# Graph attention on one core: the first batch's value blocks in bank pairs of their own, and the weights of layers two and three folded in later slots

## The reference, cut to what matters

```
xl   = x @ W1                                   # 4 heads of 128
e    = leaky_relu(asrc[:, None] + adst[None])   # asrc, adst: xl times two vectors per head
attn = softmax(where(adj > 0 or diagonal, e, -1e9), over sources)
h    = elu(attn^T @ xl + b1)                    # layer one, 4 heads
h    = attention of the same form with W2, one head of 256, + b2      # layer two
x    = layernorm(x + h)
x    = layernorm(x + leaky(softmax(masked leaky(s_i + s_j)) @ (x @ W3)))   # layer three
```

## Time and profile before

| | us |
|---|---|
| median of 3 runs | 977.99 |
| lowest, highest | 976.63, 978.44 |
| the profiled execution's own time | 977.93 |
| its span | 976.1 |

### The profile page before, as it was taken

One profiled execution on the slowest core, in us unless ns is written; L12 is line 12 of the kernel. 1 busy time (PEld: TensorE's weight loads), 2 busy tenths in 40 slices (PEclk: granted clock), 3 DMA queues, 4 the chain that ended last, 5 costly groups with the idle time before them and its releaser, 6 DMA issues.

```text
span 976.1 us, 17256 instructions
## 1 busy us (share of the span) xinstructions
PE 882.8 (90%) x6220; PEld 820.9 (84%) x6220; DVE 740.5 (76%) x1876; ACT 684.9 (70%) x1269; POOL 276.1 (28%) x255
## 2 busy tenths in 40 slices
PE   5687889999999999999999999999999999998653
PEld 4676879998999989898999989898999989897542
DVE  5657697888888887888888888888888888974430
ACT  2466858787786868787786868777786868775530
POOL 1001001124242314224242314224242314224353
PEclk9997999999999999999999999999999999999787
DMA  6303030202102030302102030302102010000000
GB/s 205 111 3 87 1 87 2 87 1 63 48 28 82 22 87 1 109 1 64 46 28 82 22 88 1 108 2 65 45 29 80 23 23 1 23 1 23 22 22 22
DMA packets 62716, 45.04 MB, mean 46 GB/s; under 512 B 35748, under 2 KB 54308, under 8 KB 62632
## 3 DMA queue, kind: packets, MB, share of 16 engines
q1 hardware_dynamic: 62632, 43.93, 15.3%
HBM read 27.14 MB, written 8.39 MB: 36 GB/s over the span
## 4 chain that ended last, share of the span: by engine, by line
PE 36%; DVE 29%; ACT 24%; issue 9%; POOL 2%; POOLq 0%; DMA 0%; SPq 0%; DVEq 0%; ACTq 0%
DVE junk L749 9%; PE bU L478 7%; PE bU L457 7%; PE bG L540 6%; PE bG L526 6%; ACT att L620 6%; ACT att L609 6%; ACT x L632 5%; DVE att L793 3%; PE bB L417 3%; DVE y_lo L786 3%; DVE low L762 3%; DVE y L774 3%; ACT att L624 2%; PE bU L468 2%
## 5 line engine op out<-in xcount | busy, mean ns | idle before, releaser
L749 DVE CUSTOM_DVE_ANT_0 junk<-mask_t,bA,val 128x512 bf16<-128x512 bf16 x320 | 219.8, 743 | 44.7 <-PE bA L417 38.2
L457 PE MATMUL bU<-val,att 128*128 128x129 f32 x2048 | 249.7, 275 | 3.3 <-DVE att L793 3.3
L457 PEld LDWEIGHTS bU<-val,att 128*128 128x128 f32 x2048 | 241.5, 192 | 5.7 <-issue 3.4
L793 DVE SCALAR_TENSOR_TENSOR att<-mask_n,att 128x2048 f32<-128x2048 bf16 x80 | 183.4, 2292 | 81.3 <-ACT att L620 81.3
L609 ACT ACTIVATE att<-bB,val 128x512 f32<-128x512 f32 x320 | 202.4, 707 | 1.3 <-PE bB L417 1.3
L620 ACT ACTIVATE att<-att 128x2048 f32<-128x2048 f32 x80 | 155.2, 1940 | 0.7
L478 PE MATMUL bU<-val3s,att 128*128 128x256 f32 x512 | 118.0, 385 | 11.8 <-POOL val3s L372 11.3
L468 PE MATMUL bU<-val,att 128*128 128x257 f32 x512 | 119.9, 388 | 9.4 <-DVE att L793 9.4
L478 PEld LDWEIGHTS bU<-val3s,att 128*128 128x128 f32 x512 | 96.2, 192 | 27.0 <-issue 13.4
L468 PEld LDWEIGHTS bU<-val,att 128*128 128x128 f32 x512 | 96.6, 194 | 23.7 <-DVE att L793 9.9
L672 ACT COPY val<-bG 128x524 f32<-128x524 f32 x64 | 38.7, 604 | 108.6 <-PE bG L540 108.6
(11 more groups left out here) (87 smaller groups left out, 1585.4 us busy)
## 6 DMA issues: line engine op xcount, KB each, us to landing
adj_in<-in_adj_dram SPq DMA_DIRECT2D x16, 1024.0 KB, 5.8
x_in<-in_x_dram SPq DMA_DIRECT2D x16, 512.0 KB, 6.7
out_dram<-act SPq DMA_DIRECT2D x16, 512.0 KB, 2.9
mask_t<-mask_n SPq DMA_TRANSPOSE x64, 2.5
att<-in_L_gnn_W_dram SPq DMA_DIRECT2D x4, 128.0 KB, 3.1
att<-in_L_gnn_W_dram SPq DMA_DIRECT2D x1, 512.0 KB, 7.4
w<-in_L_gnn_W_dram SPq DMA_DIRECT2D x1, 256.0 KB, 7.6
att<-in_L_gnn_a_dram SPq DMA_DIRECT2D x1, 256.0 KB, 7.3
```

The source lines that it names most:

```text
L457: ins = nc.tensor.matmul(to[:, (d % 2) * FX:(d % 2 + 1) * FX], p[:, s, d * P:(d + 1) * P], val1[u.batch % 2][:, s, u.index // 2, values], ...
L749: nc.vector.tensor_tensor_reduce(junk[:, b] if u.row else att[u.slot % 3][:, b], mask_t[u.batch % 4][:, b], bA[:], 1.0, a_col(u, b) if u.r ...
L793: nc.vector.scalar_tensor_tensor(flat(p), mask_n[u.batch % 3][:, 0:NB * N], BIG, flat(p), ALU.add, ALU.min)\
```

## The change

1. `fold_1` waits for each of the two spread vectors separately, and within each half of W1 it takes the four folds of the first vector before the four of the second.
2. For batch 0, blocks 1 and 2 of the values go to two pairs of banks made of bU0 to bU3, and wait for no copy. Blocks 0 and 3 stay in bG.
3. W2 is loaded into the buffer val3 and the vectors of layers two and three into val3s, instead of att1 and att2.
4. `fold_23` is cut in two. `fold_2` (eight folds) stands in slot 0 at the end of DVE's list, behind `x_low` of batch 1. `fold_3` (the low part of W2 and four folds) stands in slot 2 behind `keep_edges`.
5. ACT's copy `w2_hi` moves from slot -1 to the end of slot 1.
6. `weight_sums` moves from slot 0 to slot 3 on PE and into a bank of bG; `shift_bias_2` moves from slot 0 to slot 4 on DVE.

```
-        bU = [psum(f"bU{i}") for i in range(4)]
+        bUU = [psum(f"bUU{i}", 1024) for i in range(2)]
+        bU = [bUU[i // 2][:, (i % 2) * 512:(i % 2 + 1) * 512] for i in range(4)]
...
+        w2 = val3[:]
+        rows = val3s[:].rearrange("p k n -> p (k n)")
...
-        u_uses = [(colsum_out, 2)]
+        u_uses = []
...
             def values_1(n, b):
                 pe.wait_ge(x_lo_ready, n + 1)
+                apart = n == 0 and b in (1, 2)
                 for g in range(G):
-                    g_wait(g)
-                    to = g_bank(g)[:, 0:HX]
+                    if not apart:
+                        g_wait(g)
+                        g_free[g] = ((val1_ready, n * NB + b + 1),)
+                    to = (bU[2 * b - 2 + g] if apart else g_bank(g))[:, 0:HX]
...
             def weight_sums():
+                g_wait(0)
...
+                g_free[0] = ((colsum_out, 2),)
...
-                if g == 0:
+                if g == 3:
                     weight_sums()
...  (ACT)
-                if g == -1:
-                    act.wait_ge(folded, 2 * KD * H + G + 2 * KH)
-                    nc.scalar.copy(w2_hi[:], w2).then_inc(w2_hi_ready, 1)
...  (ACT, end of the slot, behind elu_exp)
+                if g == 1:
+                    act.wait_ge(folded, 2 * KD * H + G + 2 * KH)
+                    nc.scalar.copy(w2_hi[:], w2).then_inc(w2_hi_ready, 1)
...  (DVE, fold_1)
-                dve.wait_ge(rows_spread, 2)
+                    for i, vectors in enumerate((att1s, att1d)):
+                        dve.wait_ge(rows_spread, i + 1)
...  (DVE, the slots)
-                if g == -3:
-                    fold_23()
...
-                if g == 0:
+                if g == 4:
                     shift_bias_2()
...
                 if this and this.row:
                     keep_edges(this)
+                if g == 0:
+                    fold_2()
+                if g == 2:
+                    fold_3()
```

More of the change, by code:

```diff
@@ L143, in gat_kernel @@
         w1 = att[0][:].rearrange("p b n -> p (b n)")[:, 0:KD * G * HX].rearrange("p (k g n) -> p k g n", k=KD, g=G)
-        w2 = att[1][:].rearrange("p b n -> p (b n)")[:, 0:KH * DX].rearrange("p (k n) -> p k n", k=KH)
-        rows = att[2][:].rearrange("p b n -> p (b n)")
-        row1s, row1d = rows[0:1, 0:HF], rows[0:1, HF:2 * HF]
+        row1s, row1d = (att[2][0:1, i, :] for i in range(2))
         att1s, att1d = bU[0], bU[1]
-        att2s, att2d = rows[:, 2 * HF:2 * HF + DO], rows[:, 2 * HF + DO:2 * HF + 2 * DO]
-        att3 = rows[:, 3 * HF:3 * HF + 2 * DO]
+        w2 = val3[:]
+        rows = val3s[:].rearrange("p k n -> p (k n)")
+        att2s, att2d, att3 = rows[:, 0:DO], rows[:, DO:2 * DO], rows[:, 2 * DO:4 * DO]
         b1_in = x1[0]
@@ L541, in values_1 @@
                                                    stop=(k == KD - 1 and i == 2))
-                    g_free[g] = ((val1_ready, n * NB + b + 1),)
                 ins.then_inc(val1_done, 1)
@@ L546, in weight_sums @@
                 pe.wait_ge(folded, 2 * KD * H + G + 2 * KH)
+                g_wait(0)
                 for k in range(KH):
-                    ins = nc.tensor.matmul(bU[0][:, 0:DX], ones[:], w2[:, k], start=(k == 0), stop=(k == KH - 1))
+                    ins = nc.tensor.matmul(g_bank(0)[:, 0:DX], ones[:], w2[:, k], start=(k == 0), stop=(k == KH - 1))
                 ins.then_inc(colsum_done, 1)
+                g_free[0] = ((colsum_out, 2),)
             def spread_weights():
@@ L671, in values_1_out @@
                 act.wait_ge(val1_done, n * NB + b + 1)
-                nc.scalar.copy(val1[n % 2][:, b], bG[:].rearrange("p (g n) -> p g n", g=G)[:, :, 0:HX])\
+                banks = bUU[b - 1] if n == 0 and b in (1, 2) else bG
+                nc.scalar.copy(val1[n % 2][:, b], banks[:].rearrange("p (g n) -> p g n", g=G)[:, :, 0:HX])\
                     .then_inc(val1_ready, 1)
@@ L842, in fold_1 @@
                 dve.wait_ge(consts, 9)
-                dve.wait_ge(rows_spread, 2)
                 for k in range(KD):
                     dve.wait_ge(w1_in[k], 16 * G)
[L846 to L850, removed]
+                    for i, vectors in enumerate((att1s, att1d)):
+                        dve.wait_ge(rows_spread, i + 1)
+                        for h in range(H):
+                            g, c = h // 2, h % 2
+                            to = HC + 2 * i + c
+                            fold(w1[:, k, g, c * FX:c * FX + F], vectors[:, h * F:(h + 1) * F], w1[:, k, g, to:to + 1])
                 scores = (slice(None), slice(None), slice(None), slice(HC, HX))
@@ L870, in shift_bias_1, with fold_2 @@
                     nc.vector.scalar_tensor_tensor(to_lo, from_lo, 1.0, to_lo, ALU.add, ALU.subtract).then_inc(bias1_ready, 1)
-            def fold_23():
+            def fold_2():
                 dve.wait_ge(w23_in, 96)
@@ L876, in fold_23, with fold_3 @@
                     fold(w2[:, k, 2:DX], att2d, w2[:, k, 1:2])
+            def fold_3():
                 dve.wait_ge(w2_hi_ready, 1)
@@ L885, in shift_bias_2 @@
                 dve.wait_ge(colsum_done, 1)
-                nc.vector.tensor_copy(colsum[:], bU[0][:, 0:2]).then_inc(colsum_out, 1)
-                nc.vector.tensor_tensor(bias2[:], bias2[:], bU[0][:, 2:DX], ALU.subtract).then_inc(colsum_out, 1)
+                nc.vector.tensor_copy(colsum[:], g_bank(0)[:, 0:2]).then_inc(colsum_out, 1)
+                nc.vector.tensor_tensor(bias2[:], bias2[:], g_bank(0)[:, 2:DX], ALU.subtract).then_inc(colsum_out, 1)
                 dve.wait_ge(colsum_out, 2)
```

## The result

| | before | changed |
|---|---|---|
| median of 20 runs each, us | 977.61 | 978.99 |
| lowest to highest | 975.21 to 979.84 | 977.65 to 979.69 |
| profiled execution's own time | 977.93 | 977.65 |
| its span | 976.1 | 975.9 |

The ratio is 1.0015, with a 95% interval of 1.0008 to 1.0022: the changed kernel is 1.4 us slower. The forecast was 0.35 us faster. The two profiled executions, taken alone, say 0.3 us faster. That contradiction is the subject of what follows: the changed kernel's profiled execution is the fastest of its twenty, and those of before scatter over 4.6 us.

What follows compares the result with a forecast made beforehand. PE bounds from 140 us on; the change's worth is decided in the first 70 us, a chain of waits. Terms -1.3 - 3.4 - 3.4 - 0.6 + 3.7 + 0.45 + 1.0 + 3.0 + 0.2 = -0.35 give 977.6 us, range 976.3 to 979.0.

Steps and rivals of the forecast that it cites:

- the clock within the blocks: Batch 0's four value blocks on PE: without gaps the full clock comes inside them, 3.4 us saved.
- clock in slot 1: PE resumes earlier in slot 1 after longer idleness, and part of its work runs at half rate: +0.45 us (0 to 0.5).
- Split wait: DVE's `fold_1` at the start: four of sixteen folds leave the path, 1.3 us saved.
- Gaps: Batch 0's value blocks on PE run unbroken: each of three pitches shrinks by 1.12, 3.4 us saved.
- `fold_2` +3.7: Eight folds enter DVE's path in slot 0, between `x_low` and `tops` of head two: 3.7 us added.
- the bias shift -0.6: `shift_bias_2` leaves slot 0 on DVE: 0.6 us saved.
- `w2_hi` +1.0: The copy on ACT now stands in front of `leaky` of head two: 1.0 us added.
- `fold_3` +3.0: W2's low part and four folds on DVE, between `keep_edges` of head two and `invert` of head one: 3.0 us added.
- PE's idleness before b_t of head four: Slots 3 and 4: PE's wait grows to about 3 us, its clock may fall; 0 to +0.6, taken as +0.2 us.
- Rival A: Full clock doesn't come within the four value blocks, so 3.4 us stay away: 981.0 us, slower; chance 0.13.
- B: Later folds mostly hidden by ACT's or PE's own order at head two or three: 974.6 us, faster; chance 0.06.
- D: From 140 us PE's backlog absorbs the shift: 977.9 us, not distinguishable from the forecast; chance within the shared 0.62.

Runs made afterwards that it cites:

- the folds alone: Only the folds, `w2_hi`, weight sums and bias shift moved, on the kernel before, with fold_1's wait and the value banks as before: 982.87 against 977.22 us, 1.0065.
- the best one: Changed kernel with all twelve folds back in slot -3, `w2_hi` and W2's low part in slots 4 and 5, and added matmuls: 969.39 us, 0.9916.

## Why the prediction was wrong

**The step that failed is "the clock within the blocks", -3.4 us.** The mechanism was right: without gaps the release comes inside the blocks (3.2 to 5.4 us after the first matmul, five traces). The other side of the difference was wrong. The step took the clock of the kernel before from one execution, in which the release came at the end of the fourth block. But in four of the six traces of kernels with the gaps the release comes in the second or third block, and saves 2.8 or 4.2 us of the latest one's 15.5. Between averages, gaps and clock together are 4.1 us instead of 6.8, so the clock's part is about -0.7.

**The same mistake stands once more in the sum, in "clock in slot 1", +0.45.** Between the two first profiles the term came out exactly: batch 1's first copy is 4.21 us after b_t's spread in the changed kernel and 3.76 before. But the 3.76 was an exception. The other three traces of the kernel before have 4.21 too, so against their average (4.10) the term is +0.1.

With both terms taken between averages the sum is -0.35 + 2.7 - 0.35 = +2.0, on the side that was measured (+1.4 and +1.65 by the medians).

The anchor looked safe because the profile's own time, 977.93, was near the median. It was so by accidents that cancelled. At 127 us the profiled execution was 2.4 to 4.3 us behind the other three of the kernel before. At 134 us, where its clock fell late, it got 0.6 to 0.9 back; eleven of the thirteen other traces lose 0.6 to 1.1 us against it between 135 and 143 us. Near 875 us it got 1.2 to 1.5 back, and at the end it was 0.9 to 2.0 behind.

The prediction did have the rule. The Trainium skill (TensorE: Matmul & The Clock Gate, Part 1) says the moment of release varies from run to run, and the traces agree: 4.37, 4.37, 8.54 us and the very end for one and the same program. I wrote that the kernel before "would in some executions have its clock earlier too", and then gave this no term and no chance. It was 2.7 us of the sum.

**The other steps.**
- Split wait, -1.3: values start 1.39 us earlier; 1.9 us by the ratio.
- Gaps, -3.4: 25.06 - 15.24 = 9.82 against 20.78 - 14.00 = 6.78 us for the blocks with the clock up, 3.0. Right within 0.4.
- `fold_2` +3.7 and the bias shift -0.6: 3.73 us, lead at b_t of head two smaller by 3.1. In the second trace of the changed kernel 0.8 us come on top, beside GpSimd's instruction; the sum has no term for that.
- `w2_hi` +1.0 and `fold_3` +3.0: 0.95 and 3.00 us, with their whole length on the path, as the two waits had shown.
- PE's idleness before b_t of head four: 4.10 us, not "about 3". The clock fell in all three traces of the changed kernels (0.57 in the first); it cost between 0 and 0.5 us.
- Rival A (no release) didn't occur; by the prediction's own spacings its turning point is a release about 10 us into the blocks, not 9.7. Rival B is ruled out by the folds alone, D by the distances in the traces: in the stretch where PE is the bound, from 143 to 836 us, the distance between each trace and the first of before changes by no more than 0.4 us.

**What stays open.** The corrected sum says +2.0 and the medians +1.4 to +1.65. The averages of the traces, two of the changed kernel and four of before, differ by 2.0 us at `normalize`, 2.8 at 836 us and 1.8 in their own times: the place at 134 us takes 0.6 from the changed kernel's side, the one near 875 us gives 0.8 back. So few traces can't fix the averages better than that, and how often GpSimd's instruction meets DVE's in the changed kernel is not known either (0.8, 0.3 and 0 us in the three traces).

## What to carry to other kernels

Before a difference of a few microseconds is built on one profile, ask which of its stretches depend on the clock's state at their start, and give those an average over several executions, for the kernel before as well as for the changed one. Work that is moved off an engine's idle stretch is paid in full when the target slot lies between a wait that the engine ends and one that it causes; the rows that name the releaser on both sides tell that in advance. Idle time of PE ahead of a long matmul block can be filled with matmuls whose result isn't used: in all three traces with them the clock was up at the first value matmul, and they were worth 3.3 us in the kernel before, 1.4 us in the changed kernel and 2.7 us in the best one. And before work is moved in time on one engine, look at what the others do there: here DVE's work came beside an instruction of GpSimd's that it had not met before.

## What the runs showed of the hardware that was not expected

An instruction of DVE's can take longer when one of GpSimd's runs beside it. In the first 150 us of the fourteen traces, eight DVE instructions are more than 0.2 us longer than others of their form, and each of the eight stands beside GpSimd's mask instruction: 0.3 us in one case, 0.8 to 1.0 in the others. In six of them it fell on a fold or the low part of W2, and cost something only where no idle stretch of DVE's followed. `tops` kept its 0.74 us beside the same instruction (at 34.10 and 34.77 in the changed kernel's first trace, GpSimd from 34.40 to 35.55). Why some instructions grow longer and others not, no run here isolates.

A lead won at the start doesn't all arrive at the end, although PE is the bound for 700 us between. The version with early folds, without the added matmuls, led by 9.2 us at 135 us, by 8.3 at 836 and by 6.9 at the end. One piece went at the resumption near 134, the other near 875 us: there PE resumes after a wait, and in this execution the clock had fallen before the block. The windows of that kernel, and of the kernel before (for which the block is later by the lead):
```profile
870.00:875.00 5.00, 1.51 (x12) 0.91 0.00 0
875.00:880.00 5.00, 5.00 (x13) 0.50 0.30 105
```
```profile
880.00:885.00 5.00, 2.00 (x8) 1.00 0.00 1
885.00:890.00 5.00, 5.00 (x25) 1.00 0.30 103
```
In this execution of the kernel before the clock stays full through the same wait. Of the thirteen other traces six lost 1.2 to 1.6 us against it there, three of them the other traces of the kernel before; the other seven lost about 0.2. I take the 4 us by which executions of one kernel scatter to be the sum of such places, which the traces suggest and no run isolates.
